# Attention plus routed experts in one launch: head 1's sums folded later in five blocks, row maxima and expert tokens turned on VectorE

## The reference

```python
q, k, v = ((x @ W).reshape(b, s, H, DH) for W in (Wq, Wk, Wv))      # H = 16 heads of DH = 64
attn = softmax(einsum('bqhd,bkhd->bhqk', q, k) * DH ** -0.5)
out = einsum('bhqk,bkhd->bqhd', attn, v).reshape(b, s, H * DH) @ Wo + bo
...
expert = argmax(softmax(x @ router_w.T))                            # one of 8, for each token
out_e = square(relu(x @ fc[expert])) @ projT[expert]                # 128 -> 512 -> 128
```

## Time and profile before

| | |
|---|---|
| median of 3 runs | 1377.83 us (1377.69 to 1383.75) |
| the profiled execution | 1383.75 us, of it 1382.0 us from first to last instruction |
| PE busy | 1354.1 us, 98% |
| POOL, DVE, ACT busy | 1122.8, 1082.3, 716.9 us |
| mean granted TensorE clock | 0.984 |

### The profile page before, as it was taken

The page is one execution under the profiler, slowest core; times in us unless marked ns, Lnnn a source line. Parts: engine busy times, 40 slices in busy tenths (PEclk is TensorE's granted clock), DMA queues, the critical chain, the costliest instruction groups (busy, mean ns, idle before and its releaser), DMA issues.

```text
span 1382.0 us, 20158 instructions
## 1 busy us (share of the span) xinstructions
PE 1354.1 (98%) x6323; PEld 864.6 (63%) x6323; DVE 1082.3 (78%) x1716; ACT 716.9 (52%) x1285; POOL 1122.8 (81%) x908
## 2 busy tenths in 40 slices
PE   7999989999999999999999999999999999999998
PEld 4655656666656666656666666666667667665654
DVE  7797868777778777779777778777778777788776
ACT  4454535545555545545545546546546446555443
POOL 6679978878877879777879778779778788788986
PEclk9799999999999999999999999999999999999998
DMA  4232112221123112332114311234112331111001
GB/s 110 52 98 69 41 37 69 74 75 51 34 71 95 52 50 51 77 78 64 32 50 102 77 52 39 51 82 98 32 50 56 75 83 34 31 31 37 15 20 39
DMA packets 71706, 80.66 MB, mean 58 GB/s; under 512 B 11504, under 2 KB 40752, under 8 KB 71600
## 3 DMA queue, kind: packets, MB, share of 16 engines
q1 hardware_dynamic: 70576, 77.27, 22.3%
q0 software_dynamic: 1024, 2.10, 0.5%
HBM read 25.96 MB, written 5.24 MB: 23 GB/s over the span
## 4 chain that ended last, share of the span: by engine, by line
PE 83%; POOL 7%; DVE 6%; issue 3%; DMA 1%; ACT 0%; SPq 0%; POOLq 0%; DVEq 0%; ACTq 0%
PE OB L1158 27%; PE SB L1104 15%; PE MB L1130 14%; PE SB L1111 14%; POOL acc L527 5%; DVE mx L782 3%; PE XB L1186 2%; PE XB L1196 2%; PE XB L1092 1%; PE XB L1085 1%; PE XB L1165 1%; PE XB L1167 1%; DVE acc L805 1%; PE XB L1166 1%; POOL sorted_x L556 1%
## 5 line engine op out<-in xcount | busy, mean ns | idle before, releaser
L527 POOL TENSOR_TENSOR acc<-acc,ex 128x512 f32<-128x512 f32 x717 | 917.1, 1304 | 92.8 <-DVE acc L805 48.2
L782 DVE TENSOR_REDUCE mx<-MB 128x1 f32<-128x512 f32 x992 | 648.6, 682 | 200.7 <-PE MB L1130 197.1
L640 ACT ACTIVATE ex<-SB 128x512 f32<-128x512 f32 x1024 | 607.6, 598 | 360.2 <-PE SB L1111 298.2
L1158 PE MATMUL OB<-ex,V 128*64 128x512 f32 x2048 | 454.2, 595 | 0.0
L1104 PE MATMUL SB<-Q,K 128*128 128x512 f32 x1024 | 424.0, 414 | 0.0
L1130 PE MATMUL MB<-K,Q 128*128 128x512 f32 x992 | 395.3, 399 | 11.5 <-DVE mx L782 11.0
L1111 PE MATMUL SB<-Q,K 128*128 128x512 f32 x1024 | 403.0, 394 | 0.0
L1158 PEld LDWEIGHTS OB<-ex,V 128*64 128x64 f32 x2048 | 141.1, 137 | 277.6 <-issue 255.9
L1104 PEld LDWEIGHTS SB<-Q,K 128*128 128x128 f32 x1024 | 194.4, 190 | 94.7 <-issue 53.5
L1130 PEld LDWEIGHTS MB<-K,Q 128*128 128x128 f32 x992 | 188.6, 190 | 65.2 <-DVE mx L782 23.7
L1111 PEld LDWEIGHTS SB<-Q,K 128*128 128x128 f32 x1024 | 194.7, 190 | 32.8 <-DMA Q<-mrow 0.7
(11 more groups left out here) (137 smaller groups left out, 647.3 us busy)
## 6 DMA issues: line engine op xcount, KB each, us to landing
Q<-high SPq DMA_DIRECT2D x124, 128.0 KB, 2.3
K<-high SPq DMA_DIRECT2D x112, 128.0 KB, 2.3
Q<-low SPq DMA_DIRECT2D x64, 128.0 KB, 2.3
rd<-rows_rd SPq DMA_DIRECT2D x62, 128.0 KB, 3.0
K<-low SPq DMA_DIRECT2D x56, 128.0 KB, 2.3
w<-fc SPq DMA_DIRECT2D x23, 256.0 KB, 2.8
w<-projT SPq DMA_DIRECT2D x23, 256.0 KB, 3.1
sorted_x<-res SPq DMA_DIRECT2D x1, 1472.0 KB, 6.8
```

Source lines behind the costliest of these rows:

```text
L527: pool.tensor_tensor(a[:, :], src[:, :], EX[h][ex_slot(kt)][:, :], ALU.add).then_inc(done, 1)
L640: act.activation(EX[h][ex_slot(kt)][:, :], SB[bank_of(n, 2 * kt + h)][:, :], ACT.Exp).then_inc(a_e[h], 1)
L782: dve.tensor_reduce(mx[:, m % 2, u:u + 1], MB[bank_of(m, i)][:, :], AX.X, ALU.max).then_inc(v_m, 1)
L1158: mm = pe.matmul(OB[own[h], :], V[(n // JB) % 2][:, k, own[h]], EX[h][ex_slot(k)][:, :], start=(k == 0), stop=(k == NT - 1))
```

## The change

Three things. **(a)** `at_fold(n)` gives the key tile at which each head's sums are folded: head 0 stays at 0; head 1 goes to key tile 4 in blocks 2, 3, 29 and 30 and to key tile 2 in block 31 (0 elsewhere). In these five blocks `sum_parts` and the reciprocal follow that many key tiles later (the reciprocal at 8, and at 6 in block 31), and SP's `store_row` stands behind `spread_q`. **(b)** `nm` is padded to 32 columns, and DVE turns it with four 32x32 transposes into `mrow`, at key tile 12 behind that tile's maxima; PE's transpose and ACT's copy are gone. **(c)** SP loads a tile's tokens with four transfers that put the 32x32 squares in their turned places (in pieces of 32 numbers, 128 bytes), and one DVE transpose of 128x128 turns each square in place; this is done a block before the tile's use, in its key tile 8, and PE's transpose and ACT's copy are gone. SP's `load_tokens` stands behind `spread_rd`.

```diff
 AT_KV, AT_Q, AT_WO, AT_NM, AT_T = (1, 9), 5, 13, 11, 12
-AT_FOLD, AT_ON = 0, 10
-AT_TOK, AT_UP, AT_DOWN = 3, 4, 11
+AT_ON = 10
+AT_TOK, AT_UP, AT_DOWN = 8, 4, 11
+        def at_fold(n):
+            return 0, {2: 4, 3: 4, NB - 3: 4, NB - 2: 4, NB - 1: 2}.get(n.off, 0)
...
+                def load_tokens(r):
+                    wait(sp, v_tok, r.times(1))
+                    rows = sorted_x[bass.ds(r.place(P), P), :].rearrange("(i a) d -> a i d", a=SQ)
+                    for j in range(P // SQ):
+                        sp.dma_start(tok[j * SQ:(j + 1) * SQ, :].rearrange("a (i b) -> a i b", b=SQ),
+                                     rows[:, :, j * SQ:(j + 1) * SQ]).then_inc(d_tok, 16)
                 def load_tile(r):
                     e = sp.value_load(owner_i[0:1, bass.ds(r.place(1), 1)], min_val=0, max_val=E - 1)
-                    sp.dma_start(tok[:, :], sorted_x[bass.ds(r.place(P), P), :]).then_inc(d_tile, 16)
...
-                    if n.off:
+                    if n.off and at_fold(n)[1] == 0:
                         store_row(n - 1)
                     for kt in range(NT):
                         for m in q_jobs(n, kt):
                             spread_q(m)
                     if n.off:
+                        if at_fold(n)[1]:
+                            store_row(n - 1)
                         spread_rd(n - 1)
+                    if n.off == TILE0 - 1:
+                        for half in range(2):
+                            sp.wait_ge(d_sort[half], 16 * NT // 2)
+                        sp.wait_ge(d_res, 16)
+                    if has_tile(n + 1):
+                        load_tokens(n + 1 - TILE0)
...
-                def max_rows(m):
-                    wait(act, t_nm, m.times(1, 1))
-                    act.activation(mrow[:, :], XB[0:2 * TB, 0:P], ACT.Copy).then_inc(a_nm, 1)
...
+                def turn_max(m):
+                    wait(dve, v_nm, m.times(1, 1))
...
+                    for j in range(P // SQ):
+                        squares = slice(j * SQ, (j + 1) * SQ)
+                        ins = dve.transpose(mrow[:, squares].bitcast(F32), nm[squares, :].bitcast(F32))
+                    ins.then_inc(v_mrow, 1)
...
+                def turn_tokens(r):
+                    wait(dve, d_tok, r.times(TD, TD))
+                    wait(dve, t_up, r.times(1))
+                    dve.transpose(tokT[:, :], tok[:, :]).then_inc(v_tok, 1)
...
                     for u in range(EARLY):
                         maxima(Lin(1), u)
+                        if u == 0:
+                            turn_max(Lin(0))
...
+                        if kt == AT_T and before(n, NB - 1):
+                            turn_max(n + 1)
...
-                        if kt == AT_FOLD and not start:
-                            fold_sums(n - 1)
                         if not start:
-                            sum_parts(n - 1, kt)
+                            for h in range(2):
+                                if kt == at_fold(n)[h]:
+                                    fold_sums(n - 1, h)
+                            sum_parts(n - 1, kt - at_fold(n)[1])
...
+                        if has_tile(n + 1) and kt == AT_TOK:
+                            turn_tokens(n + 1 - TILE0)
...
-                def turn_tokens(r):
-                    take_spare(a_tok, r.times(1, 1))
-                    wait(pe, d_tile, r.times(48, 48))
-                    pe.transpose(XB[:, 0:P], tok[:, :], ident[:, :]).then_inc(t_tok, 1)
...
-                def turn_max(m):
-                    take_spare(a_nm, m.times(1, 1))
-                    wait(pe, v_nm, m.times(1, 1))
-                    pe.transpose(XB[0:2 * TB, 0:P], nm[:, m % 2, :], ident[:, :]).then_inc(t_nm, 1)
```

More of the change, by code:

```diff
@@ L212, in layer @@
         d_out = sem("d_out")
-        QD, KD = 6 * 16, 6 * 16
+        TD = P // SQ * 16
+        QD, KD, MD = 6 * 16, 6 * 16, 2 * 16
         def unit(n, kt, h):
@@ L414, in place_max @@
                     k = m % QS
-                    wait(sp, a_nm, m.times(1, 1))
+                    wait(sp, v_mrow, m.times(1, 1))
                     wait(sp, g_z, 4 + 2 * QS if m.off else 4)
@@ L918, in low_k, with fold_sums, sum_parts @@
                     dve.tensor_tensor(low[:, :], XB[:, :], high[:, :], ALU.subtract).then_inc(v_k, 1)
-                def fold_sums(n):
-                    for h in range(2):
-                        wait(dve, sums[h][n % 2], added(n, NT - 1))
-                        if h == 0:
-                            wait(dve, g_on, n.times(1))
-                        else:
-                            wait(dve, v_part, n.times(2, 1))
-                        dve.transpose(turned[:, :], acc[h][n % 2][:, :]).then_inc(v_turn, 1)
-                        wait(dve, v_turn, n.times(2, h + 1))
-                        dve.tensor_reduce(part[:, h * QB // SQ:(h + 1) * QB // SQ], turned[:, :].rearrange("p (t k) -> p t k", k=SQ),
-                                          AX.X, ALU.add).then_inc(v_part, 1)
-                def sum_parts(n, kt):
-                    if kt in (1, 2):
+                def fold_sums(n, h):
+                    wait(dve, sums[h][n % 2], added(n, NT - 1))
+                    if h == 0:
+                        wait(dve, g_on, n.times(1))
+                    else:
+                        wait(dve, v_part, n.times(2, 1))
+                    dve.transpose(turned[:, :], acc[h][n % 2][:, :]).then_inc(v_turn, 1)
+                    wait(dve, v_turn, n.times(2, h + 1))
+                    dve.tensor_reduce(part[:, h * QB // SQ:(h + 1) * QB // SQ], turned[:, :].rearrange("p (t k) -> p t k", k=SQ),
+                                      AX.X, ALU.add).then_inc(v_part, 1)
+                def sum_parts(n, step):
+                    if step in (1, 2):
                         wait(dve, v_part, n.times(2, 2))
-                        for j in (2 * kt - 2, 2 * kt - 1):
+                        for j in (2 * step - 2, 2 * step - 1):
                             ins = dve.transpose(parts[:, j * SQ:(j + 1) * SQ], part[j * SQ:(j + 1) * SQ, :])
                         ins.then_inc(v_parts, 1)
-                    if kt == 3:
+                    if step == 3:
                         wait(dve, v_parts, n.times(2, 2))
                         dve.tensor_reduce(den[:, :], parts[:, :].rearrange("t (j b) -> t b j", j=P // SQ), AX.X, ALU.add)                           .then_inc(v_den, 1)
-                    if kt == 4:
+                    if step == 4:
                         wait(dve, v_den, n.times(1, 1))
@@ L1108, in low_scores @@
                     if kt == 0 and h == 0:
-                        wait(pe, d_nm[k], (n // QS).times(32, 32))
+                        wait(pe, d_nm[k], (n // QS).times(MD, MD))
                         wait(pe, d_one[par], 32)
@@ L1240, in first @@
                             logits(c)
-                    for u in range(EARLY):
-                        max_unit(Lin(1), u)
-                    turn_max(Lin(0))
-                    for u in range(EARLY, MIDDLE):
+                    for u in range(MIDDLE):
                         max_unit(Lin(1), u)
@@ L1272, in one @@
                             project(n - 1)
-                        if kt == AT_T and before(n, NB - 1):
-                            turn_max(n + 1)
                         for m, tile, tiles in batches(n, kt):
```

47 lines of the change are left out of this document (19 added, 28 removed).

## The result

The changed kernel took 1369.62 us (median of 8 runs, 1366.69 to 1374.59), the kernel before beside it 1377.87 us (8 runs, 1377.01 to 1383.75): ratio 0.994, 95% interval 0.9923 to 0.9956, so 6.1 to 10.6 us less. Forecast were 1364 us and a range of 1358 to 1372. The profiled execution took 1368.74 us, its span is 1367.0.

What follows compares the result with a forecast made beforehand. PE, busy for 98% of the span, was taken to bound the kernel. Terms 3.6 + 1.3 + 5.8 + 3.7 - 0.5 = 13.9 us off 1383.75, moved to the median, gave 1364 us, range 1358 to 1372.

Steps and rivals of the forecast that it cites:

- rival A: The folds' stall moves to key tile 4 in blocks 29, 30 and 3, clock falling: 1371 us; chance 0.10.
- Rival B: The four transposes' lag on DVE lasts into the next block's key tile 4 in K blocks: 1370 us; chance 0.09.
- PE's two transposes: PE's stream loses the transpose of `nm` in 31 blocks and the tokens' in 11 V blocks: 4.9 us gained.
- What DVE takes over: Four 32x32 transposes at key tile 12, 0.8 us per block, are covered by DVE's permitted lag: cost 0.
- The tokens: Loads land and DVE turns them while PE is in its batch with V: cost 0 at every bound.
- Rival C: The tokens' squares, in 128-byte pieces, land late, deciding from 4.4 us behind the last issue: 1385 us; chance 0.05.
- The fold in blocks 29 and 30: Later head 1 fold removes PE's wait and slow clock, less 0.65 us waiting: 2.9 us per block, 5.8 gained.
- Block 3: Without the fold's wait the owners' search starts earlier and PE's stall shrinks from 6.34 us: 3.7 us gained (1 to 6).
- The sign named for it: In block 3, one PE stall of 1.8 us left would show the forecast right.
- Block 31: The last block makes no maxima and its end hangs on POOL's last sums: 0, within 2 us either way.
- The start: Four transposes behind one maximum hold up the first scores: 0.5 us lost (0 to 1.5).
- The move to the median: The forecast from the slowest, profiled execution, 1369.9 us, was shifted by its difference to the median 1377.83, giving 1363.9.

Runs made afterwards that it cites:

- turns_only: The changed kernel with both heads' folds at key tile 0 in all blocks, leaving only the transposes moved to DVE; 1371.35 us, ratio 0.9943.
- fold_only: The kernel before with only the late fold of head 1 in five blocks; 1375.57 us, ratio 0.9971.
- the early search: The owners' search moved from block 3 to block 1, key tile 0, in the kernel before; 1372.82 us, ratio 0.9955.

## Why the forecast held, and where it failed

The time lies in the range, 8 us lower by the medians and some 10 by the account above, where 13.9 were forecast, so the sum was too high by 4 to 5. That it lies in the range owes as much to the range's width as to the sum: two terms were off by 5.5 us together, and the measured 1369.6 is where rivals A (1371) and B (1370) had put it, though neither of them came about.

- **PE's two transposes, 4.9 us: right.** In blocks 4 to 28 the terms give 25 x 0.115 + 11 x 0.115 = 4.1; measured were 4.5. K blocks gained 0.12 each, so that the tokens' transpose was free there, V blocks 0.27. L1203 and L1079 are gone and the step is 0.23 us (286.92 to 287.15). turns_only gives 4.6 in these blocks.
- **What DVE takes over, 0: right.** Four squares took 0.83 us, and no block from 4 to 28 got longer. Rival B is out.
- **The tokens, 0: right.** In the block shown DVE waits 2.99 us for the landing and is done 1.98 before PE gives it the next unit. It waits so in 23 blocks, 82.0 us in all and at most 5.8, and none of blocks 4 to 28 shows it. The turn was 0.31 us, as taken. Median from issue to landing was 1.9 us, between the bounds. Rival C is out; its point was 4.4. The Trainium skill's read-modify-write below 512 bytes (DMA: Bandwidth & Descriptors, Specifications) stays unseen: such pieces landed in 1.9 us here, with no penalty that this kernel would feel.
- **The fold in blocks 29 and 30, 5.8 us: right in sum, not in its parts.** Of the 6.4 us some 0.2 are PE's transposes; the folds alone (fold_only) give 5.8, but 4.9 beside the early search and 4.3 beside the turns, where these two blocks had one stretch at half speed and none to lose instead of two. PE waits 0.28 us or less at key tile 4 where 0.65 was counted: rival A is out. The clock's fall was priced at 1.6 us a block, where blocks 29 and 30 without it are 0.8 and 1.1 shorter, and it isn't bound to the stall.
- **Block 3, 3.7 us: wrong, nothing gained.** The step that failed is "The owners' search would start at 175.54 (178.76 less 3.22) instead of 180.11, so PE's unit at 185.05 comes at 180.5, 4.57 earlier". The search did start early (170.30), and it then waited for POOL's adds, inside its last operation. The term took L902's 3.69 us as work, and moved it whole. It was a wait for POOL as well, and POOL's backlog after the scatters of the tokens doesn't end earlier because DVE asks earlier. With the search elsewhere the block takes 42.5. The sign named for it, one stall of 1.8 us left, was 6.32. A smaller slip: its part for the first tile's late loads was 0.8 us, where its own 7.4 less 5.3 and 0.9 give 1.2; the trace shows nothing of it, DVE waits 5.79 us for that tile, and no wait of PE follows.
- **Block 31, "0, within 2 either way": 1.7 longer, inside its bound, and it takes back most of the folds' gain.** Beside the turns, the later folds win 4.3 us in blocks 29 and 30 and lose 3.5 in block 31. PE comes there earlier, and finds DVE and POOL with the same work in turn before them; the prediction added up neither engine's adds for that block.
- **The start, -0.5: right** (3.31 to 3.82 us from the row maxima to the first L1111, L1138 in the changed kernel).
- **The move to the median** was right: the profile of before had the stretch at half speed at the start, and its first score 5.8 us later than the profile of after.

The Trainium skill has the rule for both failures (SBUF — State Buffer, Who interferes with whom): DVE and GpSimd share a pair of SBUF ports as an exclusive lock, taken by a DVE operation with two SBUF inputs, or of a kind that can, for suitable operands, use both ports, `tensor_scalar` among them, and the one that comes second stands still. The rows agree in kind: two-input adds 1.54 us each (10.80 for seven) beside POOL's and 0.77 (5.39 for seven) without, one-input transposes 0.71 beside them. They go beyond it in size: the page has the second one wait for the first instruction, and here one operation of DVE lost to five adds in a row, though by its record it began 0.56 us before the first of them (171.72 and 172.28), and to three before. Why a whole run is let through in block 3 and one operation elsewhere wasn't settled.

## What to carry to other kernels

A small operation that shows microseconds of length can be a wait: look at what the other engine ran until the moment it ended, before its length is moved as work. Where DVE and POOL both do two-input work, add up both their times for the stretch; a stall removed upstream comes back where that sum is the limit. When undoing either of two suspects changes nothing, undo both before calling them harmless.

## What the runs showed of the hardware

- The same small operation of DVE took 0.17 us, 0.70, 1.25 and 6.72 us, according to POOL's adds beside it. POOL's division took 1.29 and 3.43 us, according to DVE's.
- DVE's add with two SBUF inputs took 0.69 us by itself and 1.75 to 1.78 in turn with POOL's (block 31 of the changed kernel); POOL's took 1.27 by itself, and eight in turn with DVE's 13.12.
- Reductions from PSUM (0.68 us), one-input transposes in SBUF (0.71 us) and additions with one input from PSUM (0.69 us) kept their length beside POOL's adds.
- A stall of PE of 2.01 us left the granted clock at full speed in one execution, where one of 1.87 us was followed by 3.41 us at half speed in another.
